# A two-layer graph kernel: residual, sum and output in three tiles, a later store, another table of dense pieces, and a softmax part moved to GpSimd

## The reference, cut to what matters

```python
h = max(layernorm(x), 0)
q, k, v = h @ Wq + bq, h @ Wk + bk, h @ Wv + bv          # 16 heads of 32
x = x + softmax(where(adj, q k^T * scale, -inf)) v @ Wo + bo
h = max(layernorm(x), 0)
alpha = max((h @ wq) (h @ wk)^T, 0) * (adj != 0)
x = x + softmax(alpha, axis=1) (h @ weight)
```

## Time and profile before

| | |
|---|---|
| median of three runs | 1922.4 us |
| the profiled execution | 1918.12 us, span 1916.3 us |
| TensorE, VectorE, ScalarE, GpSimd busy | 93%, 85%, 57%, 24% |
| the chain that ended last | TensorE 50%, VectorE 28%, issue 8%, DMA 6%, ScalarE 5% |
| granted TensorE clock, mean | 0.990 |
| DMA | 142.48 MB, mean 74 GB/s |

### The profile page before, as it was taken

The page is one execution under the profiler, slowest core; times in us unless marked ns, Lnnn a source line. Parts: engine busy times, 40 slices in busy tenths (PEclk is TensorE's granted clock), DMA queues, the critical chain, the costliest instruction groups (busy, mean ns, idle before and its releaser), DMA issues.

```text
span 1916.3 us, 53466 instructions
## 1 busy us (share of the span) xinstructions
PE 1779.5 (93%) x16817; PEld 1404.2 (73%) x16817; DVE 1620.9 (85%) x4904; ACT 1087.8 (57%) x2381; POOL 452.0 (24%) x1190
## 2 busy tenths in 40 slices
PE   3789999999999999999999999999999999999986
PEld 2557777777777777777777777777777777777763
DVE  5688888988888898888888888888888888888884
ACT  2356555656565555656566565656565656656551
POOL 1022221222122222222122222212221222222111
PEclk9899999999999999999999999999999999999998
DMA  3412122222222222222222221222222222222121
GB/s 109 139 53 77 50 84 81 81 70 78 74 58 80 84 69 78 79 59 74 79 86 67 79 79 51 82 82 71 79 79 68 65 78 85 68 79 79 44 58 39
DMA packets 195401, 142.48 MB, mean 74 GB/s; under 512 B 36000, under 2 KB 167072, under 8 KB 195360
## 3 DMA queue, kind: packets, MB, share of 16 engines
q1 hardware_dynamic: 178224, 108.93, 19.9%
q10 hardware_dynamic: 17136, 33.03, 5.5%
HBM read 57.94 MB, written 16.78 MB: 39 GB/s over the span
## 4 chain that ended last, share of the span: by engine, by line
PE 50%; DVE 28%; issue 8%; DMA 6%; ACT 5%; SPq 1%; ACTq 1%; DVEq 1%; POOL 0%; POOLq 0%
PE ring L360 34%; PE turned L425 6%; DVE probs L792 6%; DMA out_dram<-x 5%; ACT probs L588 3%; PE score L410 3%; DVE probs_t_lo L800 3%; DVE x L930 2%; DVE val L891 2%; PE ring L478 2%; PE pv L443 2%; DVE work L859 2%; DVE o_sum L813 2%; DVE xa L859 2%; DVE e_lo L951 1%
## 5 line engine op out<-in xcount | busy, mean ns | idle before, releaser
L598 ACT ACTIVATE probs_t_hi<-turned 128x512 f16<-128x512 f32 x512 | 304.7, 595 | 371.5 <-PE turned L425 336.9
L588 ACT ACTIVATE probs<-probs,least 128x256 f32<-128x256 f32 x1024 | 461.3, 503 | 10.8 <-DVE least L792 10.8
L792 DVE CUSTOM_DVE_ANT_0 probs<-score,far,undo_score 128x256 f32<-128x256 f32 x1024 | 450.5, 478 | 9.6 <-DVE far L978 9.6
L1081 POOL TENSOR_TENSOR heads_out<-o_sum,o_rcp 128x64 f32<-128x64 f32 x512 | 144.6, 303 | 1150.3 <-DVE o_sum L813 1141.1
L800 DVE TENSOR_TENSOR probs_t_lo<-turned,probs_t_hi 128x512 f16<-128x512 f32 x512 | 350.3, 684 | 50.8 <-ACT probs_t_hi L598 47.3
L425 PE MATMUL turned<-ident,probs 128*128 128x128 f32 x2048 | 311.6, 275 | 42.7 <-ACT probs L588 42.7
L425 PEld LDWEIGHTS turned<-ident,probs 128*128 128x128 f32 x2048 | 244.6, 142 | 89.1 <-ACT probs L588 53.3
L410 PE MATMUL score<-stack 128*128 128x256 f16 x1024 | 197.1, 274 | 16.4 <-DMA stack<-stage 16.4
L443 PE MATMUL pv<-val,probs_t_hi 128*128 128x65 f16 x2048 | 184.7, 191 | 4.6 <-DVE o_sum L813 2.7
L445 PE MATMUL pv<-val,probs_t_lo 128*128 128x33 f16 x2048 | 178.2, 179 | 0.0
L443 PEld LDWEIGHTS pv<-val,probs_t_hi 128*128 128x128 f16 x2048 | 157.8, 97 | 11.7 <-DVE probs_t_lo L800 5.6
(11 more groups left out here) (160 smaller groups left out, 4307.8 us busy)
## 6 DMA issues: line engine op xcount, KB each, us to landing
stack<-stage SPq DMA_DIRECT2D x2048, 32.0 KB, 1.9
x<-x_dram ACTq DMA_DIRECT2D x32, 512.0 KB, 4.4
out_dram<-x SPq DMA_DIRECT2D x32, 512.0 KB, 2.9
xa<-x_dram ACTq DMA_DIRECT2D x31, 512.0 KB, 3.7
adj_in<-adj_dram SPq DMA_DIRECT2D x32, 256.0 KB, 2.9
adjt_in<-adj_t_dram SPq DMA_DIRECT2D x32, 256.0 KB, 3.0
wq_raw<-wq_dram SPq DMA_DIRECT2D x2, 512.0 KB, 6.2
wk_raw<-wk_dram SPq DMA_DIRECT2D x2, 512.0 KB, 7.9
```

Source lines behind the costliest of these rows:

```text
L588: last = nc.scalar.activation(probs[:, u % 2, q, :], probs[:, u % 2, q, :], ACT.Exp, bias=least[:, u % 2, q:q + 1], scale=-1.0)
L598: nc.scalar.activation(pH[:, u % 2, :, :], turned[u % 2][:].rearrange("p (k n) -> p k n", k=QT), ACT.Copy).then_inc(hi["p"], 1)
L792: last = nc.vector.tensor_tensor_reduce(out=probs[:, u % 2, q, :], in0=score[u % 2][:, q * NODES:(q + 1) * NODES], in1=far[:, q, :], scale ...
L1081: last = nc.gpsimd.tensor_tensor(dst, o_sum[:, pair % 2, q:q + 3:2, :], o_rcp[:, pair % 2, q:q + 3:2].unsqueeze(2).broadcast_to([P, 2, HEAD]),
```

## The change

- x is loaded into `xin` at step 4 of its own pass, its sum with the bias goes to `x1`, and the output to `xo`. ScalarE evicts `av` into `xo` with the scale, and GpSimd adds x1 at step 15. The store of `xo` is issued in the next pass, behind the stack copies of group 1 and ahead of those of group 2.
- The table is dealt anew: v1 in halves at steps 5 and 6, `g0` ahead of `h1` at step 7, `hw` behind `al`, both `av` at step 14, `v0` whole at step 15.
- The first normalise moves from VectorE to GpSimd (step 13), with the mean negated by a further small instruction; the statistics move to steps 9 and 10, and with them the Newton instructions; `far_next` moves to step 11.
- The second softmax's low half moves from VectorE to GpSimd at step 13: two scalings of 256 columns and a subtraction of 512.
- At step 0 VectorE forms the sums of the last two heads ahead of head 0's low half. Splitting of the weights in the first pass takes three pieces a step on two steps.

```diff
...
-NSTEPS = (3 + 4 * NEWTON_ROUNDS, 2 + 3 * NEWTON_ROUNDS)
+NSTEPS = (4 + 4 * NEWTON_ROUNDS, 2 + 3 * NEWTON_ROUNDS)
...
     ["qk3"],
-    ["v1", "h2_0", "h2_1"],
-    ["h1_0", "h1_1", "g0"],
+    ["v1a"],
+    ["h2_0", "h2_1", "v1b"],
+    ["g0", "h1_0", "h1_1"],
     ["g1"],
-    ["hw0"],
     ["qk0"],
     ["al"],
-    ["v0a"],
+    ["hw0"],
     ["hw1"],
-    ["v0b", "av0"],
-    ["av1", "qk1a"],
-    ["ot0", "qk1b"],
+    ["qk1"],
+    ["av0", "av1"],
+    ["ot0", "v0"],
 ]
...
-STATS1, VAR1, NORM1 = (7, 9), 9, 12
+STATS1, VAR1, NORM1 = (9, 10), 10, 13
 VAR2, NORM2 = 4, 5
-X1_STEP, KEEP_STEP, FAR_STEP = 1, 3, 10
+X1_STEP, XIN_STEP, KEEP_STEP, FAR_STEP = 1, 4, 3, 11
+FINAL = (15, 15)
...
         x1 = sb("x1", [P, QT, DIM], f32)
+        xo = sb("xo", [P, QT, DIM], f32)
+        xin = sb("xin", [P, QT, DIM], f32)
         adj_in = sb("adj_in", [P, QT, NODES], i32)
...
         rstd = [sb(f"rstd{n}", [P, QT], f32) for n in (1, 2)]
+        minus_mean = sb("minus_mean", [P, QT], f32)
         newton = [sb(f"newton{n}", [P, 3, QT], f32) for n in (1, 2)]
...
                    "hw0": (lo["hw"], 2, 0), "hw1": (lo["hw"], 2, 1),
-                   "av0": (final, 2, 0), "av1": (final, 2, 1),
+                   "av0": (weighed, 2, 0), "av1": (weighed, 2, 1),
                    "qk0": (lo["qk"], 4, 0), "qk1": (lo["qk"], 4, 1),
...
                     stack_heads(1, t)
+                if prev and started(p - 1):
+                    store(p - 1)
+                if cur:
                     stack_heads(2, t)
...
                             load_raw(sp, name, half)
-                if prev:
-                    sp.wait_ge(final, count(p, 2, 1))
-                    sp.dma_start(out_v[p, :, :, :], x1[:]).then_inc(stored, 16)
+            def store(b):
+                sp.wait_ge(final, count(b, 2, 1))
+                sp.dma_start(out_v[b, :, :, :], xo[:]).then_inc(stored, 16)
             sweep(sp, body)
+            store(BATCH - 1)
             sp.wait_ge(stored, 16 * BATCH)
...
                                          ACT.Copy).then_inc(hi["g"], 1)
+                elif name.startswith("av"):
+                    act.wait_ge(mm["av"], count(b, 2, k))
+                    if k == 0 and started(b - 1):
+                        act.wait_ge(stored, count(b - 1, 16, 15))
+                    nc.scalar.activation(xo[:, k, :], src[:], ACT.Copy, scale=undo_final[:, 0:1]
+                                         ).then_inc(weighed, 1)
...
                 present = {-1: prev, 0: cur, 1: nxt}
-                if prev:
-                    if started(p - 1):
-                        act.wait_ge(stored, count(p - 1, 16, 15))
-                    act.dma_start(x1[:], x_v[p, :, :, :]).then_inc(x1_in, 16)
                 for s in range(HEADS):
+                    if cur and s == XIN_STEP:
+                        if prev:
+                            act.wait_ge(x1_ok, count(p, 1, 0))
+                        act.dma_start(xin[:], x_v[t, :, :, :]).then_inc(x1_in, 16)
                     if cur:
...
-            def normalise(which, src, dst, b):
+            def second_normalise(b):
...
                         op0=ALU.max, op1=ALU.mult).then_inc(l1_masked, 1)
-                elif name.startswith("av"):
-                    dve.wait_ge(mm["av"], count(b, 2, k))
-                    nc.vector.scalar_tensor_tensor(out=x1[:, k, :], in0=src[:],
-                                                   scalar=undo_final[:, 0:1], in1=x1[:, k, :],
-                                                   op0=ALU.mult, op1=ALU.add).then_inc(final, 1)
...
                     nc.vector.reciprocal(l1_rcp[:], l1_sum[:]).then_inc(l1_rcped, 1)
-                if s == AL_STEP + 3:
-                    dve.wait_ge(hi["e"], count(b, 1, 0))
-                    for m in range(QT):
-                        last = nc.vector.scalar_tensor_tensor(
-                            out=eL[:, m, :], in0=work[:, 1, m * NODES:(m + 1) * NODES],
-                            scalar=l1_rcp[:, m:m + 1], in1=eH[:, m, :],
-                            op0=ALU.mult, op1=ALU.subtract)
-                    last.then_inc(lo["e"], 1)
                     if prev and s == NORM2:
-                        normalise(1, x1, work, p)
+                        second_normalise(p)
                     if prev:
                         second_softmax(s, p)
+                    if s == 0 and prev:
+                        sum_parts(HEADS // 2 - 1, p)
                     if cur:
                         turned_low(s, t)
-                    if s == 0 and prev:
-                        sum_parts(HEADS // 2 - 1, p)
-                    elif s > 0 and s % 2 == 0 and cur:
+                    if s > 0 and s % 2 == 0 and cur:
                         sum_parts(s // 2 - 1, t)
...
                         first_stats(STATS1.index(s), n + 1)
-                    if s == NORM1 and cur and later:
-                        normalise(0, xa, xa, n + 1)
                     for name in DENSE[s]:
...
             step(nc.vector.memset(tops[:], 0.0))
-            normalise(0, xa, xa, 0)
             for c in range(FIRST):
...
                 settle(pool, pool_settled)
+                step(nc.gpsimd.tensor_scalar(minus_mean[:], meanvar[0][:, :, 0], -1.0, None,
+                                             ALU.mult))
                 step(nc.gpsimd.tensor_scalar(v, meanvar[0][:, :, 1], EPS, None, ALU.add))
...
                     step(nc.gpsimd.tensor_tensor(y, y, a, ALU.mult))
+            def first_normalise(b):
+                pool.wait_ge(nstep[0], count(b, NSTEPS[0], NSTEPS[0] - 1))
+                settle(pool, pool_settled)
+                for q in range(QT):
+                    nc.gpsimd.tensor_scalar(xa[:, q, :], xa[:, q, :], minus_mean[:, q:q + 1],
+                                            rstd[0][:, q:q + 1], ALU.add, ALU.mult
+                                            ).then_inc(normed[0], 1)
+            def second_softmax(b):
+                pool.wait_ge(hi["e"], count(b, 1, 0))
+                settle(pool, pool_settled)
+                for m in range(QT):
+                    part = work[:, 1, m * NODES:(m + 1) * NODES]
+                    last = nc.gpsimd.tensor_scalar(part, part, l1_rcp[:, m:m + 1], None, ALU.mult)
+                last.then_inc(e_ok, 1)
+                pool.wait_ge(e_ok, count(b, 1, 0))
+                settle(pool, pool_settled)
+                nc.gpsimd.tensor_tensor(eL[:].rearrange("p m n -> p (m n)"), work[:, 1, :],
+                                        eH[:].rearrange("p m n -> p (m n)"), ALU.subtract
+                                        ).then_inc(lo["e"], 1)
+            def residual(k, b):
+                pool.wait_ge(weighed, count(b, 2, k))
+                nc.gpsimd.tensor_tensor(xo[:, k, :], xo[:, k, :], x1[:, k, :], ALU.add
+                                        ).then_inc(final, 1)
...
                         norm_heads(s // 2 - 1, t)
+                    if s == AL_STEP + 3 and prev:
+                        second_softmax(p)
+                    if s == NORM1 and later:
+                        first_normalise(n + 1)
+                    for k in range(QT):
+                        if s == FINAL[k] and prev:
+                            residual(k, p)
                     if s == X1_STEP and prev and not started(p - 1):
                     if s == X1_STEP and prev:
+                        if started(p - 1):
+                            pool.wait_ge(final, count(p - 1, 2, 1))
                         pool.wait_ge(x1_in, count(p, 16, 15))
                         for q in range(QT):
-                            last = nc.gpsimd.tensor_tensor(x1[:, q, :], x1[:, q, :], out_bias[:],
+                            last = nc.gpsimd.tensor_tensor(x1[:, q, :], xin[:, q, :], out_bias[:],
                                                            ALU.add)
...
             reciprocal_deviation(0)
+            first_normalise(0)
             sweep(pool, body)
```

More of the change, by code:

```diff
@@ L86 @@
 LAST_SCALE_STEP = step_of(SPARE[-1])
-assert LAST_SCALE_STEP == 13 and len(SPARE) == KT + 2 and TOP_STEP + 4 < LAST_SCALE_STEP
+assert LAST_SCALE_STEP == 14 and len(SPARE) == KT + 2 and TOP_STEP + 4 < LAST_SCALE_STEP
 def count(graph, per_graph, k):
@@ L237, in two_layers @@
         normed = [sem("normed1"), sem("normed2")]
-        far_ok = sem("far_ok")
-        head_ok = sem("head_ok")
+        far_ok, weighed = sem("far_ok"), sem("weighed")
+        head_ok, e_ok = sem("head_ok"), sem("e_ok")
         l1_topped, l1_summed = sem("l1_topped"), sem("l1_summed")
@@ L703, in body @@
                     if cur and not prev and s >= LAST_SCALE_STEP:
-                        at = EARLY + 2 * (s - LAST_SCALE_STEP)
-                        for c in range(at, at + 2):
+                        at = EARLY + 3 * (s - LAST_SCALE_STEP)
+                        for c in range(at, at + 3):
                             split_high(c)
@@ L854, in reciprocal_deviation @@
```

(16 more changed lines are left out.)

## The result

After the change the median of four runs is 2041.0 us (2040.58 to 2041.42), beside 1922.5 us for the kernel before, measured with it: a ratio of 1.0617, with a 95% interval of 1.0599 to 1.0635. The profiled execution took 2041.23 us with a span of 2039.4.

The account below looks back on a forecast made before the run. It took TensorE, 93% busy, as the bound, with VectorE's chain delaying g0. Profiled 1918.1 + 81.8 (av0's wait for GpSimd) - 0.2 - 1 = 1998.7; the median lies 4.3 higher, so 2003 us, range 1970 to 2045.

Parts of the forecast that it names:

- Part 1: Three tiles and late store: step 0 loses its 1.4 us wait for the output's store, at no cost.
- Part 3: Dense table: VectorE's chain into g0 loses 3.1 us where it lost 1.2; with the store, 0.13 us a graph gained.
- T4: Tn is the start of step n (first transposition of a head's probabilities); g0 was to start at T4 + 12.7.
- Part 4: Softmax low half on GpSimd, queued behind Newton steps, mask and head sums: av0 at step 14 waits 2.95 us.
- near 85 us in 29 places: Sign in the list of waits: TensorE's ring waiting for GpSimd's e_lo, at this total and count.
- The quick-scaling rival: GpSimd scales 256 columns in 0.36 us, so av0 waits only 2.0 us: 1975 us in all; chance 0.12.
- the mutual slowing: Rival: VectorE and GpSimd slow each other, stretching GpSimd's work by a third; wait 2.0 us longer, 2061; chance 0.13.
- Sum: Whole kernel: a graph takes 56.33 + 2.95 = 59.28 us; 29 passes add 81.8, giving 1998.7 profiled, 2003 median.
- The forecast's own range: Range of the main forecast alone, without rivals: 1985 to 2022 us, chance 0.62.
- a store's wait on ScalarE: Rival: the store's wait stays elsewhere on ScalarE, 1.4 us a graph in 29: 2044 us; chance 0.05.
- the edges: Start and end of the execution: -1 us at the start, nothing in all at the end, within 3 us.
- al ahead of hw saves perhaps 1: Term at the end of the execution: al placed before hw was to save perhaps 1 us.

Follow-up runs that it names:

- e6: Kernel before with only the separate tiles for x and output and the later store; table, softmax and normalise as before: 1893.0 us, ratio 0.9853.
- e1: Changed kernel with the softmax's low half back on VectorE at step 13: 1920.8 us, ratio 1.000.
- e4: Changed kernel with twelve further 512-column matmuls ahead of av0's wait, into av0's own bank: 2007.8 us, ratio 1.0449.
- e7: Changed kernel with the low half on VectorE, another table (steps 5 and 6 as before the change), statistics at steps 8 and 9: 1907.0 us, ratio 0.9925.
- e8: Changed kernel with the earlier table and its steps for statistics, normalise and far_next, and the low half on VectorE: 1890.0 us, ratio 0.9844.

## Why the prediction was right, and where it fell short

**Part 1, right.** Step 0 is 2.19, as predicted, and the store no longer stands among ScalarE's waits, where the earlier trace rows had it with 33.2 us. e6 shows what this is worth alone: 28 us.

**Part 3, right in size and in chain.** T4 was 748.02, so g0 starts at T4 + 12.60 (predicted 12.7), and T8 is T4 + 16.10 (16.2). Step 5 is 3.03 (3.1). VectorE's timeline answers to the earlier trace rows and, with its first and last lines, to the start and to the earlier trace rows:

```profile
48.04 0.29 DVE L980 COPY far<-far_next 128x512 bf16<-128x512 bf16 x1 [7.24 <-POOL far_next L1152]
...
755.47 0.68 DVE L815 TENSOR_TENSOR probs_t_lo<-turned,probs_t_hi 128x512 f16<-128x512 f32 x1
...
758.68 1.28 DVE L879 SCALAR_TENSOR_TENSOR h_lo<-ring,h_hi 128x512 f16<-128x512 f32 x2
759.88 0.68 DVE L906 TENSOR_TENSOR val<-ring,val 128x512 f16<-128x512 f32 x1
...
1996.68 0.75 DVE L921 SCALAR_TENSOR_TENSOR x<-ring,undo_out,x 128x512 f32<-128x512 f32 x1 [1.56 <-PE ring L369]
```

From the low halves of h2 through v1's into g0 VectorE never idles. That the new table thus loses about what the store gives (0.13 us a graph left) is what e1 measures: no change.

**Part 4, right in place and size, and in its wait.** The softmax work was to start 0.56 us after T14 and did (785.60, T14 = 785.04); it was to last 3.16 us and did. That the length came out to 0.01 us is luck, since two errors in it cancelled: a scaling is 0.92 us where 0.85 was taken, the subtraction 1.15 where it was 1.27. Step 14 is 6.41 (predicted 6.42), an undisturbed graph 59.23 (59.28). The list of waits shows the wait as predicted in size and number, 81.2 us for "near 85 us in 29 places", but under another name than e_lo. GpSimd's groups by shape (busy, mean ns, idle before), beside the earlier trace rows:

```profile
L1084 POOL TENSOR_SCALAR work<-work,l_rcp 128x256 f32<-128x256 f32 x64 | 58.5, 922 | 29.2 <-ACT e_hi L689 29.2
...
L1075 POOL TENSOR_SCALAR xa<-xa,minus_mean,rstd 128x512 f32<-128x512 f32 x64 | 49.5, 777 | 0.3 <-POOL rstd L1069 0.3
...
L1088 POOL TENSOR_TENSOR e_lo<-work,e_hi 128x512 f16<-128x512 f32 x32 | 36.9, 1153 | 5.9 <-POOL work L1084 5.9
```

The quick-scaling rival falls with the first of these rows, and the mutual slowing with GpSimd's timeline: the second head sums took 0.54, not 0.72. The Trainium skill, GPSIMD Engine Reference, section 3.1, gives 769 ns for a one-input loop over 512 elements; the normalise, 777 ns, agrees, the scaling, 922 ns for half as many, does not, and the measurement decides.

**The step that failed is "Sum".** It priced the wait as its own length, 2.95 us in 29 passes, and TensorE's work behind it at full speed. e4 shows the missing term: 33 us of TensorE at half its clock. With it, 2003 becomes 2036. In the list of rivals a fallen clock is missing too. The page of before had TensorE at a clock of 0.990, and nothing in the prediction asked what a new idle stretch of 3 us a graph would do to that.

**That the range held is partly luck.** The forecast's own range, 1985 to 2022, missed the result by 19 us. The wider range reached up to 2045 for a store's wait on ScalarE (2044), and there is no such wait: 2041 falls there by the clock and the edges, which the range was not made for.

**The edges were mis-sized too, by 11.** The profiled execution is 42.5 above the sum's 1998.7: 32.0 for the clock, 11.3 for the edges, and 0.8 less in the passes. (The median is only 38 above 2003, since before's profiled execution lay 4.3 below its median and this one does not.) At the start -1 was predicted, for VectorE's normalise; instead 3.5 us were lost up to T0 of the first graph and 2.3 in pass 0. The 1.0 us was not won, since VectorE's next work (the low half of wq) now waits 1.12 us for ScalarE. And the statistics stand behind the first evictions on VectorE, so GpSimd's Newton steps start at 39.31, before the change at 36.48, and with them the first mask is late. Where the 2.3 us of pass 0 went stays open. GpSimd's timeline, and above VectorE's 7.24 us wait for that mask at 48.04:

```profile
39.31 0.22 POOL L1059 TENSOR_SCALAR minus_mean<-meanvar 128x2 f32<-128x2 f32 x1 [25.21 <-DVE meanvar L838]
```

At the end nothing was predicted, and 4.3 us were lost. The wait for the bias sum did vanish (1.56 on TensorE at 1996.68, for the earlier trace rows's 4.32): 3.6 us fewer from T0 to there. But "al ahead of hw saves perhaps 1" was wrong: from g0 to the mask of al there are 1.7 us more. The 2.6 us of hw0 no longer lie between, but three things cost more than that. g1 now takes the bank of g0, with no h1 between them in the last pass, and idles TensorE for 1.41 us until the low half of g0 is made. al, with no hw0 ahead of it, idles it for 1.50 us until that of g1 is made (above, 2014.01 and 2018.31). And g0 itself takes 5.0 us for 4.0, as more of it falls into a stretch of halved clock. h2 is 1.2 later, the softmax on GpSimd costs 2.45 (2.4 predicted), and av with its output 2.7 (1.3 predicted), at a clock that had fallen. -3.64 + 1.66 + 1.20 + 2.45 + 2.67 gives 4.34.

## What to carry to other kernels

Work moved to an engine that is mostly idle is late by what stands ahead of it in that engine's queue: here 3 us of arithmetic cost nothing one step earlier or needed one step later, and 120 us where it stood. Price a new wait of the engine that bounds the kernel with the clock at which it resumes, not only with its length. And before a table is dealt to TensorE's pace, count the evictions of each step: in e6, e7 and e8 a part of what one step gained was given back in another.

## What the runs showed of the hardware that was not expected

- TensorE's clock fell to half (1.2 of 2.4 GHz) behind single waits of 2.8 us, once a graph of 59 us, in 19 of 27 passes, for some 3 us, and cost 1.69 us each time. In the kernel before, TensorE's longest wait in a graph is 1.2 to 1.3 us (at T0, for ScalarE's exponentials), and the clock falls in none of the passes 3 to 29. Of passes with the 2.8 us wait that look alike in the trace about one in three was spared; what decides that is open.
- On GpSimd one multiplication by a per-partition scalar over 256 columns took 922 ns, while an addition and a multiplication over 512 took 777 ns. The first works in place on half a tile whose other half VectorE uses; whether that or the form of the instruction is the cause was not tried.
